# A four-layer graph network: the last layer's attention kept within graphs and its refinement folded into other products

## The reference, cut to what matters

```
def _L3_gnn_ref(base_features, neighbor_mask, parent_child_mask, Wq, bq, Wk, bk, Wv, bv, Wo, bo, alpha, gamma):
    x = base_features
    Q = x @ Wq + bq
    K = x @ Wk + bk
    V = x @ Wv + bv
    scale = 1.0 / jnp.sqrt(jnp.asarray(K.shape[-1], x.dtype))
    scores = jnp.einsum('bnh,bmh->bnm', Q, K) * scale
    scores = scores + parent_child_mask[None] * alpha
    scores = jnp.where(neighbor_mask[None] == 0, jnp.asarray(-1000000000.0, x.dtype), scores)
    attn = jax.nn.softmax(scores, axis=-1)
    attn_out = jnp.einsum('bnm,bmh->bnh', attn, V)
    refined = attn_out @ Wo + bo + x
    child_sum = jnp.einsum('nm,bmd->bnd', parent_child_mask, refined)
    is_parent = (parent_child_mask.sum(axis=1) > 0).astype(x.dtype)
    delta = gamma * (child_sum - refined)
    return refined + delta * is_parent[None, :, None]
```

## Time and profile before

| | us |
|---|---|
| median of 3 runs | 2243.28 (2242.56 to 2246.55) |
| the profiled execution | 2243.94 |
| its span in the profile | 2242.2 |
| PE busy, of the span | 2139.0 (95%) |
| DVE, ACT, POOL busy | 62%, 52%, 23% |

### The profile page before, as it was taken

How to read it: one execution, slowest core, us unless ns; L and a number is a source line. 1 busy time by engine, 2 the same in 40 slices (tenths; PEclk the granted TensorE clock), 3 DMA queues, 4 the chain that set the end, 5 groups by cost and what they waited for, 6 DMA issues and landing times. The chain is left out here.

```text
span 2242.2 us, 44474 instructions
## 1 busy us (share of the span) xinstructions
PE 2139.0 (95%) x17363; PEld 1879.8 (84%) x17363; DVE 1388.6 (62%) x2734; ACT 1164.9 (52%) x2184; POOL 515.9 (23%) x1167
## 2 busy tenths in 40 slices
PE   6999999999969989999999999999999898989998
PEld 5898888888859978888888889978888897868886
DVE  5788888888856644443344434344443688957776
ACT  1454455445533467644444434354434576758886
POOL 3554565556530000000000000000000222015554
PEclk9999999999979999999999999999999999989999
DMA  4011111111121110000000000000000242012221
GB/s 125 16 30 40 58 41 31 46 58 34 39 104 57 56 50 19 1 19 1 1 0 20 19 1 1 1 1 19 1 1 1 81 126 76 1 33 66 75 75 52
DMA packets 76527, 82.62 MB, mean 37 GB/s; under 512 B 6624, under 2 KB 74080, under 8 KB 75488
## 3 DMA queue, kind: packets, MB, share of 16 engines
q1 hardware_dynamic: 76384, 80.53, 11.5%
HBM read 55.34 MB, written 25.17 MB: 36 GB/s over the span
## 5 line engine op out<-in xcount | busy, mean ns | idle before, releaser
L334 PE MATMUL ps<-R 128*128 128x256 f32 (+3 forms) x8136 | 1497.3, 343 | 22.1 <-DVE R L1754 8.3
L334 PEld LDWEIGHTS ps<-R 128*128 128x128 f32 x8136 | 1310.4, 190 | 184.8 <-issue 9.5
L1404 ACT ACTIVATE late_half<-ps,lstm_bias 128x512 f32<-128x512 f32 (+2 forms) x460 | 283.4, 670 | 380.6 <-PE ps L334 380.5
L376 POOL TENSOR_TENSOR ln_veps<-ln_mv,eps_tile 128x2 f32<-128x2 f32 x128 | 25.1, 196 | 1162.5 <-DVE ln_mv L359 1162.5
L304 POOL TENSOR_TENSOR H<-H 128x128 f32<-128x128 f32 x384 | 203.8, 564 | 1.4 <-DMA residual<-H 1.4
L1474 DVE TENSOR_TENSOR late_half<-late_half 128x1024 f32<-128x1024 f32 (+2 forms) x32 | 37.6, 1176 | 186.4 <-ACT late_half L1404 186.4
L895 PE MATMUL ps<-H 128*128 128x256 f32 x512 | 126.7, 391 | 10.7 <-issue 9.9
L1398 ACT ACTIVATE late_half<-late_half 128x1024 f32<-128x1024 f32 (+2 forms) x66 | 68.1, 1032 | 124.4 <-DVE late_half L1479 78.4
L919 PE MATMUL ps<-H 128*128 128x256 f32 x512 | 121.4, 383 | 0.0
L1476 DVE TENSOR_TENSOR late_half<-late_half 128x1024 f32<-128x1024 f32 (+2 forms) x32 | 37.6, 1176 | 132.6 <-ACT late_half L1404 132.6
L895 PEld LDWEIGHTS ps<-H 128*128 128x128 f32 x512 | 94.7, 195 | 23.4 <-issue 11.1
(11 more groups left out here) (213 smaller groups left out, 2739.3 us busy)
## 6 DMA issues: line engine op xcount, KB each, us to landing
H<-in_x SPq DMA_DIRECT2D x64, 256.0 KB, 2.9
residual<-H SPq DMA_DIRECT2D x32, 256.0 KB, 2.2
H<-residual SPq DMA_DIRECT2D x32, 256.0 KB, 3.9
arena<-residual SPq DMA_DIRECT2D x32, 256.0 KB, 2.7
residual<-arena SPq DMA_DIRECT2D x32, 256.0 KB, 2.2
H_state<-residual SPq DMA_DIRECT2D x32, 256.0 KB, 2.8
out<-H_state SPq DMA_DIRECT2D x32, 256.0 KB, 2.2
arena<-in_wih SPq DMA_DIRECT2D x4, 1024.0 KB, 4.9
```

What stands on the lines that cost most here:

```text
L334: mm = pe.matmul(out, lhsT(a), rhs(b), start=start and n == 0, stop=stop and n == len(PASSES) - 1)
L1404: ins = act.activation(into[q][:, m, 0:x.cols], gate_ps(q, m, x.cols), ACT.Tanh if q == TANH_G else ACT.Sigmoid, bias=lstm_bias[:, x.p - 1 ...
```

## The change

- **Scores within graphs.** The score tile is 128x64: the rows of two graphs above one another, each against its own 64 nodes. A score product has 64 stationary and 64 moving columns and writes one half of the partitions; there are four of them for two. The mask is 64 wide. Maxima, exponential, sum and scaling run over half as many elements.
- **Turn and refinement in one.** Slot 9 is one 128x128 product of both tiles' weights with `refineT` instead of two turns with the identity, so that it yields the turned R x weights.
- **Quarter-array products.** Slot 10 is eight products of 64x64 operands with 64 columns each, in place of two of 128x128. In slot 11 four products of 64x64 with 256 columns each (`refine_own` = refineT + I against x3) come ahead of the two products with Wo and add into the same PSUM tile. Slot 12's product is gone, and so are `rf`, DVE's addition to it and POOL's `x3b`. Ahead of slots 10 and 11 stands a semaphore increment on PE (`alone`).
- **Biases.** bv and bo become one row vector, rowsum(R) x (bv Wo + bo), made once at the start of layer 2's second part by one POOL, one PE and two DVE operations; slot 12 adds it. ACT's slot 10 adds nothing, but reorders.
- **Prologue.** DVE makes `refine_own` (one 128x128 addition, ahead of `late_made`); POOL makes `refine_sum`, has four memsets less and makes a narrower mask table.
- **Stores.** The rows of a tile are stored as two transfers of 64 partitions each.
- **Order.** `plan4` has other ticks and leads.

```diff
@@ (tables, on POOL and DVE in the prologue)
-            link(pool.tensor_scalar(masked, adj_bd, 0.0, -NEG, ALU.is_equal, ALU.mult))
-            link(pool.tensor_tensor(far, far, masked, ALU.add))
-            link(pool.tensor_scalar(masked, adj_bd, scal[:, 0:1], None, ALU.mult))
+            link(pool.tensor_scalar(far, adj2, 0.0, -NEG, ALU.is_equal, ALU.mult))
+            link(pool.tensor_scalar(masked, adj2, scal[:, 0:1], None, ALU.mult))
...
             link(dve.tensor_copy(refineT[:], refine_ps))
+            link(dve.tensor_tensor(refine_own[:], refine_ps, ident[:], ALU.add))
@@ (order)
     plan4 = dict(
-        period=34, lead=(0, 8, 17, 26),
-        pe={1: 19, 3: 28, 4: 30, 5: 32, 6: 35, 9: 42, 10: 44, 11: 46, 12: 48},
...
+        period=34, lead=(0, 9, 18, 26),
+        pe={1: 2, 3: 10, 4: 13, 5: 17, 6: 20, 9: 26, 10: 29, 11: 33},
...
@@ (SP)
-                    sp.dma_start(rows_of_group(out_view, s, turn), y3_t[s]).then_inc(stored[s], 16)
+                    graphs = out_graphs[bass.ds(turn * STREAMS + s, 1)].rearrange("g b i d -> i (g b) d")
+                    for n in range(TILES):
+                        sp.dma_start(graphs[:, 2 * n:2 * n + 2], y3_t[s][part_of(n)]).then_inc(stored[s], 16)
@@ (POOL)
-                if slot == 3:
-                    pool.wait_ge(x3_ready[s], turn + 1)
-                    pool.tensor_tensor(x3b_t[s], x3_t[s], over_tiles(bo3), ALU.add).then_inc(x3b_ready[s], 1)
@@ (DVE, layer 2's second part)
+            dve.wait_ge(bias_asked, 1)
+            early2.step(dve.tensor_tensor(last_bias, bias_ps, last_bias, ALU.add))
+            early2.settle()
+            early2.step(dve.tensor_scalar(last_bias, last_bias, refine_sum[:, 0:1], None, ALU.mult))
+            early2.settle()
@@ (DVE, layer 3)
-                if slot == 11:
-                    dve.wait_ge(wo3_done[s], turn + 1)
-                    dve.wait_ge(x3b_ready[s], turn + 1)
-                    dve.tensor_tensor(rf_t[s], token_major(s, 0), x3b_t[s], ALU.add).then_inc(rf_ready[s], 1)
                 if slot == 12:
-                    dve.wait_ge(child_done[s], turn + 1)
-                    c.step(dve.tensor_tensor(y3_t[s], token_major(s, 1), x3_t[s], ALU.add))
-                    c.settle()
+                    dve.wait_ge(rows_done[s], turn + 1)
+                    dve.wait_ge(stored[s], 32 * turn + 32)
+                    dve.tensor_tensor(y3_t[s], row_tiles(s), over_tiles(last_bias), ALU.add).then_inc(rows_taken[s], 1)
+                    dve.wait_ge(rows_taken[s], turn + 2)
@@ (PE, slots 6, 9, 10, 11, 12)
                     for n in range(TILES):
-                        q = slice(n * P, (n + 1) * P)
-                        mm = pe.matmul(token_major(s, 0, P)[:, n, :], qk3[s][:, 0, q], qk3[s][:, 1, q],
-                                       start=False, stop=n == TILES - 1, skip_group_check=True)
+                        for g in range(2):
+                            q = slice(g * P + NODES * n, g * P + NODES * (n + 1))
+                            mm = pe.matmul(score_tiles(s)[part_of(g), n, :], qk3[s][:, 0, q], qk3[s][:, 1, q],
+                                           start=False, stop=n == TILES - 1, skip_group_check=True)
...
-                    for n in range(TILES):
-                        mm = pe.transpose(token_major(s, 0, P)[:, n, :], bd3[s][:, n, :], ident[:])
-                    mm.then_inc(at3_turned[s], 1)
+                    pe.matmul(turned_pair(s), at3_pair[s], refineT[:], start=True, stop=True)\
+                      .then_inc(at3_turned[s], 1)
...
-                    for n in range(TILES):
-                        mm = pe.matmul(token_major(s, 1, P)[:, n, :], v3[s][:, n, :], atT3[s][:, n, :],
-                                       start=True, stop=True)
+                    alone(pe, waits_passed)
+                    for g in range(2):
+                        for n in range(TILES):
+                            for c in range(2):
+                                mm = pe.matmul(value_tiles(s)[part_of(c), n, part_of(g)],
+                                               v3[s][part_of(n), g, part_of(c)], atT3[s][part_of(n), part_of(g)],
+                                               start=True, stop=True)
...
-                        mm = pe.matmul(token_major(s, 0)[:, n, :], atT3[s][:, n, :], Wo3[:], start=True, stop=True)
-                    mm.then_inc(wo3_done[s], 1)
-                if slot == 12:
-                    pe.wait_ge(rf_ready[s], turn + 2)
-                    for n in range(TILES):
-                        mm = pe.matmul(token_major(s, 1)[:, n, :], refineT[:], rf_t[s][:, n, :], start=True, stop=True)
-                    mm.then_inc(child_done[s], 1)
+                    alone(pe, waits_passed)
+                    for g in range(2):
+                        for n in range(TILES):
+                            pe.matmul(row_tiles(s)[part_of(n), g, :], refine_own[part_of(g), part_of(g)],
+                                      x3_t[s][part_of(g), n, :], start=True, stop=False, skip_group_check=True)
+                    for g in range(2):
+                        mm = pe.matmul(row_tiles(s)[:, g, :], oT3[s][:, g, :], Wo3, start=False, stop=True,
+                                       skip_group_check=True)
+                    mm.then_inc(rows_done[s], 1)
```

More of the change, by code:

```diff
@@ L436, in build_program @@
     big = sq(P)
-    masked, far = sq(P), sq(P)
+    masked, far = sq(NODES), sq(NODES)
     ones = sq(P)
@@ L1597, in build_program @@
     db = region(H2_words)
-    x3, xT3, x3b, xr = ([db(G2) for _ in S] for _ in range(4))
+    x3, xT3, y3, xr = ([db(G2) for _ in S] for _ in range(4))
     qk3 = [db(2, GROUP) for _ in S]
-    v3 = [db(TILES, ATT3) for _ in S]
-    bd3 = [db(TILES, P) for _ in S]
-    atT3 = [db(TILES, P) for _ in S]
-    hs3 = [db(KD, GROUP) for _ in S]
-    rf_t = [tiles_of(v.rearrange("p a n -> p (a n)")) for v in qk3]
-    x3_t, x3b_t, xr_t, y3_t = ([tiles_of(v) for v in b] for b in (x3, x3b, xr, xT3))
+    v3 = [db(2, ATT3) for _ in S]
@@ new lines, in build_program, with score_tiles, turned_pair, value_tiles @@
+    at3 = [db(TILES, NODES) for _ in S]
+    at3_pair = [v.rearrange("p n k -> p (n k)") for v in at3]
+    atT3 = [db(P) for _ in S]
+    oT3 = [db(TILES, P) for _ in S]
+    hs3 = [db(KD, GROUP) for _ in S]
+    bv_rows = adjT[:]
+    last_bias = bo3
+    bias_ps = ps[:, 7, 0:D]
+    x3_t, y3_t, xr_t = ([tiles_of(v) for v in b] for b in (x3, y3, xr))
+    def score_tiles(s):
+        return token_major(s, 0, NODES)
+    def turned_pair(s):
+        return half(s, 0)[:, 3 * P:4 * P]
+    def value_tiles(s):
+        return ps[:, BANKS * s:BANKS * (s + 1), D:D + P]
@@ L1625, in _ @@
         def _(sp):
-            ahead(sp, stored, by=16)
+            ahead(sp, stored, by=32)
             for b in range(BUFS):
@@ L1728, in stage @@
                     act.wait_ge(at3_turned[s], turn + 1)
-                    act.activation(atT3[s], token_major(s, 0, P), ACT.Copy).then_inc(atT3_ready[s], 1)
+                    act.activation(atT3[s], turned_pair(s), ACT.Copy).then_inc(atT3_ready[s], 1)
                 if slot == 10:
                     act.wait_ge(o3_done[s], turn + 1)
-                    act.activation(atT3[s], token_major(s, 1, P), ACT.Identity, bias=bv3_col[:, 0:1])\
+                    act.activation(oT3[s].rearrange("p g (n i) -> p n g i", n=TILES),
+                                   value_tiles(s).rearrange("p n (g i) -> p n g i", g=2), ACT.Copy)\
                        .then_inc(o3T_ready[s], 1)
@@ L1782, in _ @@
             steps = Steps(dve, "p9_dve", {1: 1 + LN_STATS, 8: 2})
-            tail = Steps(dve, "p9_dve_tail", {12: 1 + LN_STATS})
-            ahead(dve, rf_ready)
+            tail = Steps(dve, "p9_dve_tail", {12: LN_STATS})
+            ahead(dve, rows_taken)
             def stage(s, slot, turn):
@@ L1820, in _ @@
         def _(pe):
+            pe.wait_ge(l3_loaded, 5 * 16)
+            pe.wait_ge(bv_made, 1)
+            pe.matmul(bias_ps, bv_rows, Wo3, start=True, stop=True).then_inc(bias_asked, 1)
             for g in range(WIDES):
@@ L1851, in stage @@
                     pe.wait_ge(hn_ready[s], turn + 1)
-                    pe.wait_ge(rf_ready[s], turn + 1)
+                    pe.wait_ge(rows_taken[s], turn + 1)
                     for n in range(TILES):
```

60 lines of the change are left out of this document (30 added, 30 removed).

## The result

The changed kernel takes **2250.31 us** (median of 8 runs, 2248.48 to 2254.02), the kernel before 2244.07 beside it (8 runs, 2242.56 to 2247.83): ratio 1.0028, 95% interval 1.0019 to 1.0036. So it is slower, by 6.2 us, where 2232 was forecast, and it lies outside the range of 2225 to 2247. The profiled execution took 2251.16, with a span of 2249.4.

The account below looks back on a forecast made before the run. PE was taken to bound layer 3. Groups falling from 7.05 to 6.73 us, times 32, gave 10.2; plus 2.0 drain, less 0.3 prologue, 11.9 off 2243.94: 2232 us (2228 to 2236 at 0.50; with most rivals 2225 to 2247).

Parts of the forecast that it names:

- The change lies in layer 3 ... and all but a few operations of it: Scope: the effect was summed per group of layer 3, against 7.05 us, times 32, plus small terms at the ends.
- PE's products: Layer 3, per group: kept slots 4.36, mask and slot 9 0.51, scores 0.60, slot 10 0.45, slot 11's quarters 0.81; sum 6.73 us.
- the price taken from layer 0: Switching into and out of a quarter-product block on PE, read from layer 0's rows: 0.38 us per block.
- So no wait has to stay.: Layer 3: ACT at 5.4 and DVE's loop at 5.9 fit under 6.73, so all waiting goes: 10.2 us gained.
- a new wait takes the place of the old: Rival: DVE's loop through ACT misses its place by a 1.0 us step, period 6.9 us; 2238 us, chance 0.12.
- Drain: 2.0: End of layer 3: twice, quarters at 0.81 replace the `rf` wait of 0.78 and 1.13 of work; 2.0 us gained (0 to 3).
- Fill: "I count nothing": Start of layer 3: its chain of turn, statistics, root, turn, Q and K stays, so no gain was counted.
- Prologue: +0.3: Ahead of layer 0's first product: one DVE operation of 0.29 and its handover before `late_made` add 0.3 us.
- The bias row: Layer 2's second part: PE's product and DVE's two short operations are hidden; uncovered they would cost about 1 us.
- two at a time: Rival: slot 11's 256-column quarters run in pairs, stream 0.86, +0.43 per group; 2246 us, chance 0.08.
- one after another: Rival: slot 11's 256-column quarters run singly, stream 1.73, group 8.03 us; 2274 us, chance 0.12 including like-sized stalls.
- scores one by one: Rival: the scores' two column halves don't run side by side, +0.22 us per group; 2239 us, chance 0.12.

Follow-up runs that it names:

- e11: Kernel before with 32 unused bytes between R2 and late_half, so only late_half (gates and cells) moved; 2244.5 us, ratio 1.0002.
- e1: Kernel before with one unused 128x1 tensor, so R2 starts 32 bytes higher, at 163488; 2257.66 us, ratio 1.0061.
- e9: Kernel before with 32 unused bytes between H and R, moving R and R2 up together, their distance kept; 2244.7 us, ratio 1.0003.
- e10: Kernel before with R 32 bytes up and the arena 8 words shorter, so R2 stays at 163456; 2262.81 us, ratio 1.0087.

## Why the prediction was wrong

By its own steps:

- **"The change lies in layer 3 ... and all but a few operations of it", and with it the sum.** This is the step that failed. The sum counted what the change does and not where it puts things. Among its edits was a tensor of one word, and its price, +13.2 us, is more than the whole gain forecast. Without it the change takes 2235.3 us: inside the range, 3 us from the forecast, but that closeness is luck, since two errors of layer 3 (below: PE's products 0.22 a group too dear, a wait of 0.39 taken for none) nearly cancel. No row of before shows this; what could have been seen is that R2 is allocated behind the tensors that the change adds and shrinks.
- **PE's products: 6.73 a group, and 6.51 measured.** Kept slots 4.36, counted as forecast. Slots 9, 3, 1 and the mask take 1.37 together, so beside the 0.88 of slots 3 and 1 some 0.49 is left for slot 9 and the mask (0.51). Slot 4's row, 1.92, holds 0.19 over its 1.73, which belongs to the switches on both sides of it; I split it as in layer 0, 0.10 for leaving slot 10 and 0.09 for entering slot 11. Slot 11's quarters are then 0.592 + 0.09 + 0.10 = 0.79 (0.81), and scores and slot 10 0.38 + 0.39 + 0.10 = 0.87, against 0.60 + 0.45 = 1.05. The scores' stream was right (0.23 for 0.22); with slot 10's left at 0.22, which was not measured, the switching was 0.42 instead of 0.61: going from the mask to the scores and from these to slot 10 is cheaper than the price taken from layer 0, which holds for a way in and a way out with 128x128 products on both sides. The rule of the Trainium skill, "TensorEngine Tiling (Array Packing)", Key Properties, that was weighed there (a change of tiling mode drains the engine) agrees with the 0.36 us of slot 11; it gives no size.
- **"So no wait has to stay."** Wrong by 0.39 us a group, 12.5 us in 32 (layer 3 is 240.1 - 228.7 = 11.4 us longer for it). The loops of DVE and ACT were priced and were indeed under the period, as 6.51 without a wait shows. What was not looked at is a counter that two slots add to. Their order on POOL was turned round by the change, and the order rows of POOL, which the text did not show, were the place to see it. The rival "a new wait takes the place of the old" gives nearly the right period (6.9) by luck: it added 0.2 to a sum that was 0.22 too high, where the wait was 0.39, and it named DVE's loop through ACT, which was not it.
- Together layer 3 as changed gained 29 x (7.05 - 6.90) = 4.5, 1.6 in its fill and 1.4 in its drain, 7.5 in all; forecast was 12.2 (10.2 + 2.0). With the counter mended it gains 247.6 - 228.7 = 18.9.
- **Drain: 2.0, and 1.4 measured.** The wait for `rf` went, but PE now waits for ACT's copy ahead of the quarters:

```profile
2236.22 0.66 PE L1935 MATMUL ps<-H_state,refine_own 64*64 64x256 f32 x8 [0.60 <-ACT H_state L1752]
...
2239.67 0.66 PE L1935 MATMUL ps<-H_state,refine_own 64*64 64x256 f32 x8 [0.58 <-ACT H_state L1752]
```

- **Fill: "I count nothing", 1.6 measured**, from the first turn to the third group's slot 4 (22.13 to 20.56). Which edit brings it was not tried.
- **Prologue: +0.3.** `refine_own`'s row is 0.29 as forecast; the product starts 1.39 later than in the earlier trace rows, the rest from `lnormT`. By 660 us the two traces are 0.6 apart, and it does not show in the time.
- **The bias row:** hidden, as forecast, as far as the traces tell: layer 3 of the kernel with the old address starts within their spread, 0.8 us earlier than before.
- The rivals on the quarters (two at a time, one after another) and on the scores one by one fall with the doubled sets (+0.43 and +0.23).

## What to carry to other kernels

Ask of a change what it allocates, not only what it runs: print the addresses before and after, and keep the distance between the tensors that TensorE reads together. A stage whose code is the same and whose start drifts has to be compared by the distance between starts of like instructions; a busy share of 100% says nothing about the pace. And where two steps add to one counter, their order is part of every wait on it: when a change turns that order round, the wait asks for both.

## What the runs showed of the hardware

- The pace of float32r products with a new weight load each depends on the distance in SBUF between the stationary and the moving operand: 226.7 to 233.3 ns for 512 columns, 206.7 to 211.8 for 462, 188.9 to 193.3 for 420. Distances that differ by 256 or 512 bytes gave the same pace, and no distance tried is best for all three. How the two reads get in each other's way was not shown, nor whether it needs both to be float32r. The Trainium skill, "SBUF — State Buffer", Who interferes with whom, gives TensorE an independent read port for weight loads and says that it waits for nobody. No wait for another engine shows here either (e11 moved what those work on, to no effect), but by these runs the pace of TensorE hangs on both of its read addresses together (e1, e9, e10), which speaks against two reads that don't touch each other.
- Four 64x64 products with 256 columns, with four different moving operands, take 0.43 us together, as long as one; four products of 128 rows with 64 columns, in pairs side by side, 0.23. Entering and leaving the 64x64 form cost 0.36 us around slot 11; the three changes of form from the mask through scores and slot 10 to slot 4 cost some 0.42 together, an estimate that leaves slot 10's stream at 0.22.
- `lnormT` on VectorE, 128x128, took 0.35 to 1.57 us. In all 20 traces it ended 0.14 to 0.15 us behind a GpSimd subtraction that was under way when it began: 1.52 and more beside the long one of 2.35 us (28.45 to 30.80 in the changed kernel, `lnormT` to 30.94), 0.35 to 0.46 where one of 1.26 us was nearly done (28.01 to 29.29 in the kernel before, `lnormT` to 29.44). The Trainium skill, "SBUF — State Buffer", Who interferes with whom, says that a VectorE instruction with two SBUF inputs and a GpSimd instruction that reads SBUF block each other; these rows agree.
